# Attention with one-pass spread of the inverse denominators, and denominators right behind the value products

## What is computed

```
q = x @ wq.T + bq;  k = x @ wk.T + bk;  v = x @ wv.T + bv          # q: 32 heads, k and v: one
weights = softmax(where(causal, q k^T / sqrt(32), -inf))
x1 = layernorm(x + (weights @ v) @ wo.T + bo)
y  = fp8-scaled, clipped x1 @ weight, scaled back
out = layernorm(x1 + y)
```

## Time and profile before

| | us |
|---|---|
| median of 3 runs | 2510.32 (2508.66 to 2511.88) |
| the profiled execution, its own time | 2512.94 |
| its span in the trace | 2511.2 |
| TensorE busy, share of the span | 2408.2, 96% |
| VectorE busy | 1750.0, 70% |
| ScalarE busy | 1299.4, 52% |
| GpSimd busy | 802.8, 32% |

### The profile page before, as it was taken

How to read it: one execution, slowest core, us unless ns; L and a number is a source line. 1 busy time by engine, 2 the same in 40 slices (tenths; PEclk the granted TensorE clock), 3 DMA queues, 4 the chain that set the end, 5 groups by cost and what they waited for, 6 DMA issues and landing times.

```text
span 2511.2 us, 36167 instructions
## 1 busy us (share of the span) xinstructions
PE 2408.2 (96%) x14312; PEld 1559.2 (62%) x14312; DVE 1750.0 (70%) x1294; ACT 1299.4 (52%) x1412; POOL 802.8 (32%) x441
## 2 busy tenths in 40 slices
PE   6999999699999999999999999999999995999998
PEld 5888887245555555555555555555555554888887
DVE  6334335798887888888888888888788884444444
ACT  2222223576777777777776776777777662000000
POOL 2232221022232322232223232322233232556653
PEclk9999999899999999999999999999999997999999
DMA  7433433342232122212222222122212211222221
GB/s 235 142 117 138 154 126 122 94 119 60 74 64 50 43 64 55 54 43 64 51 56 43 52 57 64 43 52 56 65 43 64 51 68 67 84 89 91 88 87 64
DMA packets 150742, 198.01 MB, mean 79 GB/s; under 512 B 8558, under 2 KB 108878, under 8 KB 148558
## 3 DMA queue, kind: packets, MB, share of 16 engines
q1 hardware_dynamic: 126990, 144.71, 22.2%
q10 hardware_dynamic: 23616, 51.39, 5.3%
HBM read 123.72 MB, written 72.35 MB: 78 GB/s over the span
## 4 chain that ended last, share of the span: by engine, by line
PE 66%; DVE 7%; ACT 5%; issue 3%; POOL 1%; ACTq 0%; DVEq 0%; POOLq 0%
PE bank L1233 18%; PE bank L1245 16%; PE bank L1308 14%; PE bank L1218 12%; DVE acc L1000 6%; ACT prob L761 4%; PE bank L1255 2%; PE bank L1263 2%; PE bank L1298 1%; PE bank L1215 1%; ACT att_hi L748 0%; DVE res L974 0%; DVE stats L816 0%; DVE r_den L961 0%; POOL prob L609 0%
## 5 line engine op out<-in xcount | busy, mean ns | idle before, releaser
L761 ACT ACTIVATE prob<-bank 128x1024 f32<-128x1024 f32 x1088 | 1054.9, 1022 | 442.2 <-PE bank L1233 435.3
L1000 DVE TENSOR_TENSOR acc<-acc,prob 128x2048 f32<-128x2048 f32 x420 | 988.3, 2353 | 107.0 <-ACT prob L761 88.7
L1233 PE MATMUL bank<-q_st,keys 98*128 98x512 f32 x2176 | 644.8, 415 | 33.6 <-ACT prob L761 22.1
L1233 PEld LDWEIGHTS bank<-q_st,keys 98*128 98x128 f32 x2176 | 377.0, 189 | 367.9 <-ACT prob L761 264.0
L1245 PE MATMUL bank<-prob,v_t 128*32 128x512 f32 x4352 | 526.3, 602 | 0.0
L609 POOL TENSOR_SCALAR_AFFINE_SELECT prob<-prob 128x1024 f32<-128x1024 f32 x128 | 184.1, 1461 | 736.2 <-ACT prob L761 736.2
L1245 PEld LDWEIGHTS bank<-prob,v_t 128*32 128x32 f32 x4352 | 114.0, 109 | 263.6 <-issue 253.0
L996 DVE TENSOR_TENSOR acc<-prob 128x2048 f32<-128x2048 f32 x60 | 137.6, 2293 | 153.9 <-ACT prob L761 139.5
L1132 PE MATMUL bank<-xt_hi,w_hi 128*128 128x512 f32 x576 | 227.6, 395 | 14.8 <-DVE xt_lo L837 14.1
L1132 PE MATMUL bank<-xt_hi,w_lo 128*128 128x512 f32 x576 | 227.1, 394 | 0.0
L1132 PE MATMUL bank<-xt_lo,w_hi 128*128 128x512 f32 x576 | 226.7, 394 | 0.0
(11 more groups left out here) (112 smaller groups left out, 2555.9 us busy)
## 6 DMA issues: line engine op xcount, KB each, us to landing
q_st<-q_hi_d SPq DMA_DIRECT2D x128, 256.0 KB
xt_raw<-x_t SPq DMA_DIRECT2D x16, 1024.0 KB, 6.9
q_hi_d<-part_hi ACTq DMA_DIRECT2D x64, 256.0 KB, 2.1
q_lo_d<-part_lo ACTq DMA_DIRECT2D x64, 256.0 KB, 2.3
q_st<-q_lo_d SPq DMA_DIRECT2D x64, 256.0 KB
res<-x SPq DMA_DIRECT2D x32, 512.0 KB, 6.0
x_d<-res SPq DMA_DIRECT2D x32, 512.0 KB, 2.7
x<-x_d SPq DMA_DIRECT2D x32, 512.0 KB, 3.3
```

Source lines behind the costliest of these rows:

```text
L761: nc.scalar.activation(prob[:, s % SLOTS, 2 * p:2 * p + 2], bank[:, 2 * p:2 * p + 2], ACT.Exp, scale=SCALE).then_inc(p_done, 1)
L1000: nc.vector.tensor_tensor(acc[:, n % 2], acc[:, n % 2], new, ALU.add).then_inc(acc_done, 1)
L1233: last = nc.tensor.matmul(bank[:, g].rearrange("p (a n) -> p a n", n=P), keys[:, k // QT, k % QT * P:(k % QT + 1) * P], queries[:, :, g], ...
```

## The change

- `denominators(n)` moves from between the two `scores` to the end of a batch, right behind the value products. `den_at` becomes `(begins + lengths + 1) // 2`: for a group that ends at an even step this is a batch earlier, otherwise the same batch.
- `invert(n)` stands behind VectorE's sum of an odd step, and has two more instructions: `r_hi` is the reciprocal cut to float32r, and `r_parts` holds in the upper four of a denominator's eight partitions the reciprocal (rounded by the write) and in the lower four the rest, by a column `r_lower` of 0 and -1 that is made once at the start.
- `spread` becomes float32r with two ones per column, at an upper and a lower copy, so `spread_out` is four one-pass products that add both parts. It stands two batches behind the denominators instead of one. `normalise_group` stands a step later, at odd steps.
- `att_hi` and `att_lo` become two each, by `q % 2`. ScalarE's cut waits for the projection of the tile two before. The second pair lies where the early `wf` pieces 2 and 3 lay, so these are now loaded behind the last step, when the next to last tile's projection is over.
- The table of places: a pair's long tile begins its projection two steps later (8 for 6, end 22 for 20), the short one's cut stands at 13 for 21, and its second half is spread over five batches (32 to 40) for four. Rows of x are loaded where a projection begins instead of where the cut is made.

The diff, cut to its core:

```diff
-spread = sb("spread", [P, QT, P])
+spread = sb("spread", [P, QT, P], F32R)
+r_lower = sb("r_lower", [P, 1])
...
-    s.enter_context(nc.sbuf_tensor("w_lo_rest", [P, D - 2 * P], F32))
+    r_hi = sb("r_hi", [P, P], F32R, s)
+    r_parts = sb("r_parts", [P, P], F32R, s)
+    s.enter_context(nc.sbuf_tensor("w_lo_rest", [P, D - 4 * P], F32))
...
-    s.enter_context(nc.sbuf_tensor("wo_stage_rest", [P, 2 * D], F32))
+    att_hi0 = sb("att_hi0", [P, KT, P], F32R, s)
+    att_lo0 = sb("att_lo0", [P, KT, P], F32R, s)
...
-    att_hi = sb("att_hi", [P, KT, P], F32R, s)
-    att_lo = sb("att_lo", [P, KT, P], F32R, s)
+    att_hi1 = sb("att_hi1", [P, KT, P], F32R, s)
+    att_lo1 = sb("att_lo1", [P, KT, P], F32R, s)
...
+    att_hi, att_lo = (att_hi0, att_hi1), (att_lo0, att_lo1)
...
-    at = (begins[n] + lengths[n] + 2) // 2
+    at = (begins[n] + lengths[n] + 1) // 2
...
-        names = (21, 24, 30, 30, 32, 38, 38, 39, 44, 45) if second else (4, 6, 12, 12, 14, 20, 20, 22, 27, 28)
+        names = (13, 24, 30, 30, 32, 40, 40, 41, 46, 47) if second else (4, 8, 14, 14, 16, 22, 22, 23, 28, 29)
...
-        names = (17, 20, 24, 24, 26, 30, 30, 31, END, END) if second else (4, 6, 10, 10, 12, 16, 16, 18, 22, 23)
+        names = (11, 20, 24, 24, 26, 30, 30, 31, END, END) if second else (4, 8, 12, 12, 14, 18, 18, 19, 23, 24)
...
+row_at = {places(q)[HALF0 if q < LAST_A else SPLIT]: q for q in range(LAST_B)}
...
                 sp.dma_start(wf_sim_d[:, k], piece).then_inc(piece_sent, 16)
-        if s in split_at:
-            q = split_at[s]
+        if s in row_at:
+            q = row_at[s]
...
             store_row(scale_at[s - 1])
-        if s == 2 * PAIR:
-            sp.wait_ge(piece_sent, 16 * KT)
-            load_wf(2)
-            load_wf(3)
...
+    sp.wait_ge(y_done, 2 * LAST_A + 2)
+    load_wf(2)
+    load_wf(3)
...
-    nc.gpsimd.memset(spread[:], 0.0).then_inc(fixed, 1)
+    nc.gpsimd.memset(kv[:, TB - 1], 0.0).then_inc(fixed, 1)
...
-    nc.gpsimd.affine_select(out=spread[:].rearrange("p c (h d) -> p (c h) d", d=HD), in_=spread[:].rearrange("p c (h d) -> p (c h) d", d=HD),
+    nc.gpsimd.affine_select(out=kv[:, TB - 1].rearrange("p (g d) -> p g d", d=HD), in_=kv[:, TB - 1].rearrange("p (g d) -> p g d", d=HD),
...
+    pool.wait_ge(fixed, 3 + HG)
+    nc.gpsimd.affine_select(out=kv[:, TB - 1].rearrange("p (g d) -> p g d", d=HD), in_=kv[:, TB - 1].rearrange("p (g d) -> p g d", d=HD),
+                            compare_op=ALU.not_equal, fill=1.0, base=-(REPS // 2), pattern=[[-REPS, QT * HG], [0, HD]], channel_multiplier=1).then_inc(fixed, 1)
+    pool.wait_ge(fixed, 4 + HG)
+    nc.gpsimd.tensor_copy(spread[:].rearrange("p c n -> p (c n)"), kv[:, TB - 1]).then_inc(fixed, 1)
...
-        act.wait_ge(y_done, 2 * q)
-        nc.scalar.activation(att_hi[:], att[:, q % TILES_KEPT], ACT.Copy).then_inc(att_hi_cut, 1)
+        act.wait_ge(y_done, max(2 * q - 2, 0))
+        nc.scalar.activation(att_hi[q % 2][:], att[:, q % TILES_KEPT], ACT.Copy).then_inc(att_hi_cut, 1)
...
+    dve.wait_ge(consts, 6)
+    nc.vector.tensor_reduce(r_lower[:], ident[:].rearrange("p (a s i) -> p a s i", s=2, i=REPS // 2)[:, :, 1], AX.XY, ALU.add).then_inc(lower_rows, 1)
+    dve.wait_ge(lower_rows, 1)
+    nc.vector.tensor_scalar(r_lower[:], r_lower[:], -1.0, None, ALU.mult).then_inc(lower_rows, 1)
+
...
         dve.wait_ge(den_done, n + 3)
-        nc.vector.reciprocal(r_den[:], bank[:, DEN_BANK, 0:P]).then_inc(den_read, 1)
+        nc.vector.reciprocal(r_den[:], bank[:, DEN_BANK, 0:P]).then_inc(den_inverse, 1)
+        dve.wait_ge(den_inverse, 2 * n + 1)
+        nc.vector.tensor_copy(r_hi[:], r_den[:]).then_inc(den_inverse, 1)
+        dve.wait_ge(den_inverse, 2 * n + 2)
+        nc.vector.scalar_tensor_tensor(out=r_parts[:], in0=r_hi[:].bitcast(F32), scalar=r_lower[:], in1=r_den[:], op0=ALU.mult, op1=ALU.add).then_inc(den_read, 1)
...
                 nc.vector.tensor_tensor(acc[:, n % 2], acc[:, n % 2], new, ALU.add).then_inc(acc_done, 1)
-        if s % 2 == 0 and s // 2 in group_of_den:
+        if s % 2 == 1 and s // 2 in group_of_den:
             invert(group_of_den[s // 2])
-        if s % 2 == 0 and s // 2 - 1 in group_of_den:
+        if s % 2 == 1 and s // 2 - 1 in group_of_den:
...
-            last = nc.tensor.matmul(dst, (att_hi, att_lo)[a][:, k], (wo_hi, wo_lo)[c][:, k, cols],
+            last = nc.tensor.matmul(dst, (att_hi, att_lo)[a][q % 2][:, k], (wo_hi, wo_lo)[c][:, k, cols],
...
         for c in range(QT):
-            last = nc.tensor.matmul(bank[:, DEN_BANK, c * P:(c + 1) * P], spread[:, c], r_den[:], start=True, stop=True)
+            last = nc.tensor.matmul(bank[:, DEN_BANK, c * P:(c + 1) * P], spread[:, c], r_parts[:], start=True, stop=True)
...
-        if u in group_of_den:
-            denominators(group_of_den[u])
-        if u - 1 in group_of_den:
-            spread_out(group_of_den[u - 1])
+        if u - 2 in group_of_den:
+            spread_out(group_of_den[u - 2])
...
             weigh_values(2 * u - 1)
+        if u in group_of_den:
+            denominators(group_of_den[u])
...
     half_projection(LAST_A, 0, 0, 2)
```

More of the change, by code:

```diff
@@ L65, in build @@
     REPS = HD // HG
-    FIXED = 4 + HG
+    FIXED = 6 + HG
     LN = 6
@@ L228, in build @@
         den_read = sem("den_read")
+        den_inverse = sem("den_inverse")
+        lower_rows = sem("lower_rows")
         spread_done = sem("spread_done")
@@ L613, in _ @@
                     pool.wait_ge(att_hi_cut, q + 1)
-                    nc.gpsimd.tensor_tensor(att_lo[:], att[:, q % TILES_KEPT], att_hi[:].bitcast(F32), ALU.subtract).then_inc(att_cut, 1)
+                    nc.gpsimd.tensor_tensor(att_lo[q % 2][:], att[:, q % TILES_KEPT], att_hi[q % 2][:].bitcast(F32), ALU.subtract).then_inc(att_cut, 1)
                 if s in deviation_at:
@@ L705, in upper_wo @@
                 nc.scalar.activation(wo_hi[:, k], wo_stage[:, k % 4], ACT.Copy).then_inc(wo_hi_cut, 1)
+            act.wait_ge(fixed, FIXED - 1)
             add_bias(TB - 1, G, 0)
@@ L935, in _ @@
             dve.wait_ge(wo_cut, KT)
+            dve.wait_ge(lower_rows, 2)
             dve.wait_ge(flag_ready, 1)
@@ L1031, in _ @@
             dve.wait_ge(att_hi_cut, LAST_B + 1)
-            nc.vector.tensor_tensor(att_lo[:], att[:, LAST_B % TILES_KEPT], att_hi[:].bitcast(F32), ALU.subtract).then_inc(att_cut, 1)
+            nc.vector.tensor_tensor(att_lo[LAST_B % 2][:], att[:, LAST_B % TILES_KEPT], att_hi[LAST_B % 2][:].bitcast(F32), ALU.subtract).then_inc(att_cut, 1)
             for i in range(1, 4):
```

## The result

| kernel | median us | lowest to highest | runs |
|---|---|---|---|
| before | 2509.49 | 2508.30 to 2511.88 | 4 |
| changed | 2493.14 | 2490.14 to 2495.77 | 4 |

The changed kernel takes 0.9933 of the time (95% interval 0.9916 to 0.9951): 16 us faster, where 60 were forecast. It lies outside the range of 2434 to 2480 us. The profiled execution of the changed kernel has a span of 2490.7 us, 20.5 us under the one of before.

What follows compares the result with a forecast made beforehand. TensorE, busy 96% of the span, was taken as the bound. Gains of 13 + 27.5 + 7 + 8 + 4.5 = 60 us led from a median of 2510.3 us to 2450 us, range 2434 to 2480 us.

Steps and rivals of the forecast that it cites:

- Denominators: TensorE's denominators moved behind the value products: both idles go, 0.86 us each, 54 us for 67, gain 13 us.
- spread: TensorE's spread in four one-pass records, 0.56 us for 1.01 to the next product: gain 27.5 us, bounds 34 and 4.
- load-limited choice: Spread records on TensorE limited by their unchanged weight load: 0.56 us for four, against 0.34 by columns and 1.01 unshortened.
- the rule: TensorE's batch: 5.19 us plus 0.23 per product over six, at least 5.36, plus bias, denominators, spread; excess is time over it.
- no shorter: Rival: one pass of the spread is no shorter, its gain falls from 27.5 to 4 us, 2474 us; chance 0.10.
- limited by columns: Rival: no new waits and a spread limited by columns, 7 us and 7 us more, 2436 us; chance 0.13.
- Places: New table of projection places: what certain TensorE batches cost over 5.36 us falls from 19 to 12 us, gain 7 us.
- It hides, with little to spare, and costs nothing but the waits above: VectorE's added work, 2 us per pair: 91 us of VectorE stand against about 96.5 us of TensorE in a pair.
- Waits: TensorE's waits: 6 us for `att_lo` and 9 us for sums and reciprocal go, 7 us of new ones come, gain 8 us.
- Tail: Behind the loop: the wait for the last `att_lo` and the half clock go, with 0.4 us from the spread, gain 4.5 us.
- VectorE becomes the bound in places: Rival: new VectorE waits at 15 pairs, `wf` pieces and first pair give back 20 us, 2470 us; chance 0.17.

Runs made afterwards that it cites:

- e6: Changed kernel with the residual added ahead of VectorE's sum over keys, the short tile's largest at step 49 for 47 and its cut four steps later: 2448.64 us.
- e8: e6 with the float32 spread in four passes and the reciprocal alone on VectorE: 2473.99 us.
- e3: Changed kernel with the float32 spread in four passes and the reciprocal alone on VectorE: 2491.84 us.
- e2: Changed kernel with the table of places of the kernel before: 2478.38 us.
- e9: Changed kernel with only the short tiles' cut and largest at later steps, the residual still behind the sum over keys: 2479.74 us.
- e1: Changed kernel with VectorE's residual addition ahead of the step's sum over keys instead of behind it: 2465.68 us.
- e11: Changed kernel with GpSimd's subtraction for `att_lo` doing one of eight blocks from the third tile on, the rest left out: 2460.91 us.

## Why the prediction was wrong

By its own steps:

- **Denominators** (13 us) and **spread** (27.5 us): right as prices of TensorE. 6.25 us for 6.22 and 0.57 for 0.56 in the rows; 25.3 us for the spread in e6 against e8. The load-limited choice was right over both ends. The Trainium skill (TensorE: Matmul & The Clock Gate, Back-to-back issue gap) gives 81 ns a pair, from which 0.43 us is an estimate; this trace has 0.57 us. e3 shows that in this kernel the spread's gain was not had.
- **The sums themselves**: the rule, applied batch by batch, gives 15.5, 29.9 and 2.3 us for denominators, spread and places where the forecast has 13, 27.5 and 7; the total, 47.7, is nearly the same, so this split was off and the sum right. By the forecast's own counts the spread's bounds are 39 and 0.5 us, not 34 and 4, so "no shorter" meant 2477 us and "limited by columns" 2431 us, outside the range; and 0.43 us would add 8 us and not 5.
- **Places** (7 us): wrong in sign for the whole. The table as it stands cost 14.8 us (e2). It puts the cut of the short tile and its largest next to a bank that must be freed at once; moving these two alone gave 13.4 us (e9).
- **"It hides, with little to spare, and costs nothing but the waits above"** (VectorE): this step failed. It compared VectorE's busy time in a pair with TensorE's and took room on average for being in time. The added work was priced near enough (0.23 and 0.35 us alone, with the gaps 0.6 for 0.5 us; 0.36 and 0.41 us in the mean), and the sum over a pair was not exceeded: in e6 the same 1424 instructions keep VectorE busy for 1830.9 us and TensorE never waits on `res`. What it left out is where the work stands in VectorE's order, a sum of 2.29 us ahead of the residual (27.5 us, e1), and that GpSimd's work on SBUF makes VectorE stand still at that very place (up to 32.2 us, e11). The trace of before showed the second, in rows that I had not read so: the sums over keys are 2353 ns in the mean and 2292 in the median, and one `att_lo` took 4408 ns for 2384 in the median.
- **Waits** ("14 x 0.2 us" for `add_residual`): the term in which this arrived. It was named for the short tile's first half and priced at 2.8 us; it was 35 waits and 33.6 us, and with the clock behind them the 29 batches that begin a long tile's halves carry 42.8 us of excess. Old waits fell away as forecast. This term is in the main the miss of 43 us: the excess was to fall by 8 and rose by 35.
- **Tail** (4.5 us): 4.5.
- The rival nearest to the truth was "VectorE becomes the bound in places", with 20 us given back; 43 were. It had the engine and not the place: TensorE did not follow VectorE's pace but met it at one bank, 35 times.

The forecast's 2450 us is what the program takes once that bank is freed in time (e6, 2448.64 us). I take this as a test of the sum, not as a defence of the forecast; e6 has another order and other places than the forecast kernel and an excess of 10.7 us for the 13.5 forecast, so that the two agree within 2 us is in part luck.

## What to carry to other kernels

When a change adds work to an engine that "has room", look for the one buffer that it frees just before it is used, and count what stands ahead of it in that engine's own order; moving one short instruction ahead of a long one was worth more here (27.5 us) than the whole change (16 us). Look where GpSimd's work on SBUF falls beside VectorE's, and compare means with medians of equal instructions in the trace of before: here a mean above the median was an engine that stood still. Don't add that time to busy time, which holds it already; e6 has more of it than the changed kernel, at places where it costs nothing. And test a part of a change both in the kernel as it is and in one where nothing is late: the one-pass spread was worth 0 us in the first and 25 in the second.

## What the runs showed of the hardware

That VectorE and GpSimd exclude each other for whole instructions was not in my sum, and its size is the surprise: the 29 subtractions cut short in e11, some 60 us of GpSimd's busy time, cost VectorE 40.5 us and the kernel 32.2. An instruction that reads PSUM only, the reciprocal, was not held up (0.96 us at the most). After a wait of 1.77 us TensorE went on at a granted clock of 0.51 for 3.2 us, so this wait cost nearly twice its own length; after two others of 1.67 and 1.69 us the clock stayed at 1.00.
